# The squares of the expert rows move from GpSimd to ScalarE in a fused attention and mixture-of-experts kernel

## Chip, cores and metric

The kernel runs on one core of one Trainium2 chip. The metric is the device time of one execution in microseconds (us). Time before: 830.14 us, the median of 3 runs (828.5 to 830.5). Engines are named as in the profile: PE is TensorE (PEld its weight loads), DVE is VectorE, ACT is ScalarE, POOL is GpSimd, SP is SyncE.

## The reference, cut to what matters

The layer adds two branches to x of shape (1, 2048, 256), both computed from the layer norm xn of x. The attention branch holds a fast-weight memory that is updated after every 128 rows by five Newton-Schulz steps on three 64 x 64 matrices per head, and a sliding-window attention. The other branch is a routed mixture of 32 experts with a shared expert. The routed part is the one that the change touches:

```
def relu2(x):
    return jnp.square(jax.nn.relu(x))
...
x_lat = x @ fc1_w.T
h = relu2(jnp.einsum('tl,eil->eti', x_lat, w1))
h = h * cw.T[:, :, None]
y_lat = jnp.einsum('eti,eli->tl', h, w2)
routed = y_lat @ fc2_w.T
shared = relu2(x @ shared_up_w.T) @ shared_down_w.T
```

All data is float32.

## The kernel before

**Tiles.** The 2048 rows are worked in 16 tiles of 128 rows. The program of each engine is written out by hand, one block per engine, each with a function body(i, last) that is called for each tile i. Fifteen tiles have the full body, in which the projections and the routing of the next tile m = i + 1 are prepared beside the work of tile i; the last tile has a shorter one. Every engine works strictly through its own order, and waits on counting semaphores (wait_ge) stand in front of the instructions.

**The backbone of a tile** is the fast-weight update: k_side and grads give gradients, x_first scales them to X for two groups g of heads, and five Newton-Schulz iterations follow, each in four stages st. At stage 0 TensorE turns X (ns_turn, lines 699 and 700) and ScalarE copies the result to SBUF (xt, written XT<-CC); at stage 1 TensorE makes Gram products from XT (ns_gram, CC<-XT), which VectorE copies to Am; at stages 2 and 3 TensorE makes two more products (CC<-Am, CC<-X,Mp) and VectorE makes Mp and the next X, with GpSimd's aX = a * X as its addend. After the last iteration VectorE updates and renormalises the weights Wn (update, renorm), TensorE turns them (turn_w) and ScalarE copies them to WT (w_T). Everything else is hung between the stages by a table `fill` in each engine's body: `fill = {1: [...], 2: [...]}` names what is issued after stage 1, stage 2 and so on, 20 stages in all.

**The experts** go in eight steps u of four experts each. For each step:
- TensorE: h_up(i, u) writes 128 x 512 to the one PSUM bank HB; it waits for e_hr, the relu of the step before.
- ScalarE: h_relu(i, u) writes HB to the SBUF tile hr[u % 2] and counts e_hr.
- GpSimd: h_sq(i, u) squares it to hq[u % 2] and counts e_hq. It waits for e_hr, and for e_y of step u - 2, because y_down(i, u - 2) reads the buffer that it overwrites.
- TensorE: y_down(i, u) multiplies hq with the second expert weights into the one PSUM bank YB and counts e_y. It waits for e_hq and for e_acc of the step before.
- ScalarE (y_first, step 0) or VectorE (y_acc, line 1328) adds YB, times the routing weight, to acc and counts e_acc.

The steps are spread over the stages. Where they stand decides what waits for what, so here is the order in the full body. On TensorE:

```
h_up(i, 3)
fill = {2: [lambda: q_out(i), lambda: prep_turn(m)], 3: [lambda: y_down(i, 2)],
        4: [lambda: prep_qk(m)], 5: [lambda: prep_qk_more(m)], 6: [lambda: prep_v(m)],
        7: [lambda: h_up(i, 5)], 8: [lambda: y_down(i, 3), lambda: prep_mom(m)],
        9: [lambda: prep_turn_v(m), lambda: h_up(i, 6)], 10: [lambda: y_down(i, 4)],
```

with y_down(i, 1) right after the first ns_turn of group 0 and h_up(i, 4) right after the first ns_gram of group 0; y_down 5, 6 and 7 come after stages 13, 15 and 17. On ScalarE, before the stages: k_side, gate_sig, y_first(i), h_relu(i, 2), shared_relu(i), h_relu(i, 3); then

```
fill = {1: [lambda: h_relu(i, 4)], 2: [lambda: q_out(i), lambda: prep_xnT(m)],
        5: [lambda: prep_qk(m)], 6: [lambda: prep_v(m)], 7: [lambda: h_relu(i, 5), lambda: prep_small(m)],
        8: [lambda: prep_sq8(m)], 9: [lambda: prep_vT(m), lambda: h_relu(i, 6), to_exp],
```

where the xt copies of an iteration stand at its stage 0, that is before fill 0, 4, 8, 12 and 16; h_relu(i, 7) follows stage 14. After the stages come h_relu(m, 0), y_T(i), h_relu(m, 1) and w_T. to_exp and to_sigmoid (lines 567 and 570) load ScalarE's tables for exp and ln, and those for sigmoid.

Names in rows: to and tsq are q_out's copies (VectorE's q_ms, line 1199, reads tsq), xnT is prep_xnT's, M<-wall is the projection of the next tile (it reads xnT), sgs is prep_small's sigmoid (prep_mom on TensorE and the routing read it), sq<-sl is prep_sq8's square (VectorE's prep_ss8, line 1020, reads it), gs is a step of the routing (line 1272), dhb and dga are products of k_side on VectorE (lines 1094 and 1088) that the gradients read. Line 426 is ScalarE's helper a(), line 629 TensorE's helper mm(), line 285 GpSimd's power().

Of the kernel before, what the change touches and what calls it, by code (L numbers as in the profile page):

```python
# [27 lines left out]
ALU = mybir.AluOpType  # L28
ACT = mybir.ActivationFunctionType
# [17 lines left out]
NU = E // EU  # L47
# [26 lines left out]
def build(nc, x, wall_d, rows_d, wo, fast_d, affine_d, fc1T, fc2T, e1T, e2T, upT, downT, ident_d, fixed_d, out):  # L74
# [3 lines left out]
    with ExitStack() as ctx:  # L78
        def sb(name, shape):
            return ctx.enter_context(nc.sbuf_tensor(name, shape, F32))  # L80

        def bank(name):
            return ctx.enter_context(nc.psum_tensor(name, [P, 512], F32))

        def sem(name):
            return ctx.enter_context(nc.semaphore(name))
# [102 lines left out]
        hr = [sb(f"hr{b}", [P, EU, P]) for b in range(2)]  # L189
        hq = [sb(f"hq{b}", [P, EU, P]) for b in range(2)]  # L190
# [11 lines left out]
        HB = bank("HB")  # L202
# [30 lines left out]
        e_h, e_hr, e_hq, e_y, e_acc = (sem(n) for n in ("h", "h_relu", "h_sq", "y", "acc"))  # L233
# [41 lines left out]
        @block.gpsimd  # L275
        def _(pool):

            win_scores = Expect(pool, e_as, "win_scores", first=2)
            win_pv = Expect(pool, e_av, "win_pv", first=2)
            win_raw = Expect(pool, e_rawv, "win_raw", first=3)  # L280
            win_vw = Expect(pool, e_win, "win_vw", first=5, step=2)
            pool.wait_ge(e_init, 1)

            def power(dst, src, expo, n):
                return pool.tensor_tensor(dst, src, expo[:, 0:n], ALU.pow)  # L285

            def prep_rstd(m):
                pool.wait_ge(e_veps, m + 1)
                power(rstd[:, 0:1], rstd[:, 1:2], neghalf, 1).then_inc(e_rstd, 1)

            def prep_n8(m):
                pool.wait_ge(e_ss8, m + 1)
                power(r8[:, 1, :], r8[:, 0, :], half, 8).then_inc(e_n8, 1)

            def prep_kl(m):

                pool.wait_ge(e_lr, m + 1)
                for g in range(G):
                    pool.wait_ge(e_dw[g], m)
                kk = qkn[:, D:2 * D].rearrange("p (h c) -> p h c", c=HD)  # L300
                vv = sl[:, 2 * D:3 * D].rearrange("p (h c) -> p h c", c=HD)
                for dst, src, n in ((kl0, kk, 0), (kl2, kk, 2), (vl1, vv, 1)):
                    ins = pool.tensor_tensor(dst[:, :, :], src, lr[:, :, n:n + 1].to_broadcast([P, NH, HD]), ALU.mult)
                ins.then_inc(e_kl, 1)

            def window(m, known):

                if known:
                    pool.wait_ge(e_as, m)
                    pool.wait_ge(e_av, m)  # L310
                    pool.wait_ge(e_rawv, m + 1)
                else:
                    win_scores.wait()
                    win_pv.wait()
                    win_raw.wait()
                pool.tensor_copy(akT[:, :, 0, :], akT[:, :, 1, :])
                pool.tensor_copy(vw[:, 0, :], vw[:, 1, :]).then_inc(e_win, 1)

                if known:
                    pool.wait_ge(e_win, 2 * m + 1)  # L320
                else:
                    win_vw.wait()
                pool.tensor_copy(vw[:, 1, :], raw[:, 2 * D:3 * D]).then_inc(e_win, 1)

            def restore_mask():

                pool.wait_ge(e_sm, 1)
                pool.wait_ge(e_later, 16 * NLATER)
                pool.tensor_copy(mask[:, 0, :], mask_prev[:, :]).then_inc(e_mask, 1)

            def k_u(i, g):
                pool.wait_ge(e_kc[g], i + 1)
                pool.tensor_tensor(kt[g][:, 3, :], ks[g][:, 1, :], ks[g][:, 2, :], ALU.mult).then_inc(e_ku[g], 1)  # L333

            def ss_pow(i, g):
                pool.wait_ge(e_sst[g], 3 * i + 1)
                power(r3[g][:, 2, :], r3[g][:, 1, :], half, 3).then_inc(e_pw[g], 1)

            def ax(i, g, it):
                pool.wait_ge(e_x[g], (NI + 1) * i + it + 1)  # L340
                pool.tensor_tensor(aX[g][:, :, :].rearrange("p w c -> p (w c)"),  # L341
                                   X[g][:, :, :].rearrange("p w c -> p (w c)"), a_tile[:, it, :],
                                   ALU.mult).then_inc(e_ax[g], 1)

            def row_pow(m, g):

                pool.wait_ge(e_rn[g], m + 1)
                power(r3[g][:, 4, :], r3[g][:, 3, :], half, 3).then_inc(e_rp[g], 1)

            def rms_pow(i):  # L350
                pool.wait_ge(e_msq, 2 * i + 2)
                power(r4[:, 1, :], r4[:, 0, :], neghalf, 4).then_inc(e_rms, 1)

            def shared_sq(i):
                pool.wait_ge(e_ur, i + 1)
                pool.tensor_tensor(us[:, :, :], ur[:, :, :], ur[:, :, :], ALU.mult).then_inc(e_us, 1)

            def h_sq(i, u):
                pool.wait_ge(e_hr, NU * i + u + 1)
                if u > 1 or not (isinstance(i, int) and i == 0):  # L360
                    pool.wait_ge(e_y, NU * i + u - 1)
                b = u % 2
                pool.tensor_tensor(hq[b][:, :, :], hr[b][:, :, :], hr[b][:, :, :], ALU.mult).then_inc(e_hq, 1)  # L363

            def body(i, last):
                if last:
                    h_sq(i, 1)
                    h_sq(i, 2)
                    shared_sq(i)
                    h_sq(i, 3)  # L370
                    rms_pow(i)
                    for u in range(4, NU):
                        h_sq(i, u)
                    return
                m = i + 1
                first = i == 0
                k_u(i, 0)
                k_u(i, 1)
                h_sq(i, 1)
                for g in range(G):  # L380
                    ss_pow(i, g)
                prep_rstd(m)
                h_sq(i, 2)
                fill = {0: [lambda: shared_sq(i)], 1: [lambda: h_sq(i, 3)], 3: [lambda: rms_pow(i)],
                        4: [lambda: h_sq(i, 4)], 9: [lambda: prep_n8(m), lambda: h_sq(i, 5)],
                        12: [lambda: h_sq(i, 6)], 14: [lambda: h_sq(i, 7)], 16: [lambda: window(m, first)],
                        17: [lambda: prep_kl(m)]}
                if first:
                    fill[13] = [restore_mask]
                for st in range(4 * NI):  # L390
                    if st % 4 == 0:
                        for g in range(G):
                            ax(i, g, st // 4)
                    for f in fill.get(st, []):
                        f()
                for g in range(G):
                    row_pow(m, g)
                h_sq(m, 0)

            prep_rstd(0)  # L400
            for g in range(G):
                row_pow(0, g)
            prep_n8(0)
            window(0, True)
            prep_kl(0)
            h_sq(0, 0)

            body(0, False)
            for i in range(1, LAST):
                body(i, False)  # L410
            body(LAST, True)


        @block.scalar
        def _(act):
# [9 lines left out]
            def a(out_, in_, func, **kw):  # L425
                return nc.scalar.activation(out_, in_, func, **kw)  # L426
# [80 lines left out]
            def h_relu(i, u):  # L507
                act.wait_ge(e_h, NU * i + u + 1)
                if u > 1 or not (isinstance(i, int) and i == 0):
                    act.wait_ge(e_hq, NU * i + u - 1)  # L510
                a(hr[u % 2][:, :, :].rearrange("p s t -> p (s t)"), HB[:, :], ACT.Relu).then_inc(e_hr, 1)

            def y_first(i):

# [453 lines left out]
        def _(dve):  # L968
# [165 lines left out]
            def ns_m(i, g, it):  # L1134

                _, b, c = NS[it]
                dve.wait_ge(e_prod[g], 3 * NI * i + 3 * it + 2)
                nc.vector.scalar_tensor_tensor(Mp[g][:, :, :].rearrange("p w c -> p (w c)"),  # L1138
                                               Am[g][:, :, :].rearrange("p w c -> p (w c)"), b / c, CA[g][:, 0:3 * HD],
                                               ALU.mult, ALU.add).then_inc(e_mp[g], 1)  # L1140
# [313 lines left out]
```

## Time and profile before

| | before |
|---|---|
| median of 3 runs | 830.14 us |
| profiled execution, time | 830.14 us |
| its span | 828.1 us |
| PE busy | 780.7 us (94%) |
| DVE busy | 714.6 us (86%) |
| POOL busy | 406.8 us (49%) |
| ACT busy | 354.0 us (43%) |
| squares of expert rows on POOL | 128, 137.1 us |
| relus of expert rows on ACT | 128, 76.1 us |
| mean granted PE clock | 0.996 |

The span is the time from the first to the last instruction of the profiled execution; the time of the execution is 2.04 us longer. An engine's busy time says how much of the span it works, not whether the span would be shorter if it worked less: for that one needs the chain that ended last and the waits in the timeline of a single tile. A timeline row gives the start in us from the span's start, the duration in us, engine, line, operation, output<-inputs and count; brackets hold how long the engine was idle before it and whose result ended that. Consecutive like instructions are merged in one row.

### The profile page before, as it was taken

What the parts mean: (1) busy time and instruction counts of PE and PEld (TensorE: products, weight loads), DVE (VectorE), ACT (ScalarE), POOL (GpSimd) and SP (SyncE); (2) the same over time, 40 slices, a digit from 0 to 9 for tenths busy, and PEclk for the clock granted to TensorE, in tenths of its full rate; (3) what the DMA queues carried; (4) which work ended last, traced back from release to release, by engine and by line L of the source; (5) the groups of instructions that cost most, each with busy time, mean ns of one, the idle gap of its engine ahead of it and who ended that gap; (6) DMA issues with size and microseconds to landing.
All of it is one profiled execution on the core that took longest, in us unless ns stands there. A gap on an engine that the chain in (4) does not pass through costs nothing.

```text
span 828.1 us, 24889 instructions
## 1 busy us (share of the span) xinstructions
PE 780.7 (94%) x9776; PEld 668.5 (81%) x9776; DVE 714.6 (86%) x2592; ACT 354.0 (43%) x868; POOL 406.8 (49%) x535
## 2 busy tenths in 40 slices
PE   3899999999999999999999999999999999999997
PEld 1888888888888888878888788887888888888886
DVE  4789898898988979889798897988979889898876
ACT  2544344443444434444344444444444444434533
POOL 1654555445454454544555445544465444655442
PEclk9899999999999999999999999999999999999999
DMA  8100000000000000000000000000000000000000
GB/s 321 54 3 14 9 2 21 3 13 9 2 21 2 14 8 2 21 2 15 8 3 20 2 15 9 3 21 2 15 8 2 21 2 15 8 2 15 2 15 7
DMA packets 9811, 15.09 MB, mean 18 GB/s; under 512 B 1120, under 2 KB 8928, under 8 KB 9440
## 3 DMA queue, kind: packets, MB, share of 16 engines
q1 hardware_dynamic: 7904, 7.80, 3.2%
q10 hardware_dynamic: 1792, 5.70, 1.8%
q8 instruction: 78, 1.28, 0.6%
q14 instruction: 37, 0.30, 0.1%
HBM read 11.41 MB, written 2.10 MB: 16 GB/s over the span
## 4 chain that ended last, share of the span: by engine, by line
PE 53%; DVE 33%; issue 6%; ACT 5%; POOL 2%; DMA 1%; SPq 0%; DVEq 0%
PE CC L629 18%; PE M L629 13%; PE HB L629 8%; DVE acc L1328 8%; PE YB L629 8%; DVE Wn L1175 4%; DVE Mp L1138 2%; DVE dhb L1094 2%; DVE X L1146 2%; PE CC L699 2%; DVE Am L1131 2%; POOL r L285 2%; DVE sm L1233 1%; DMA rows<-in_rows 1%; PE CC L700 1%
## 5 line engine op out<-in xcount | busy, mean ns | idle before, releaser
L363 POOL TENSOR_TENSOR hq<-hr 128x512 f32<-128x512 f32 x128 | 137.1, 1071 | 71.9 <-ACT hr L426 71.9
L285 POOL TENSOR_TENSOR r<-r,half 128x3 f32<-128x3 f32 (+1 forms) x78 | 77.9, 1011 | 155.1 <-DVE r L1116 67.9
L629 PE MATMUL HB<-xlT,e_s 128*128 128x128 f32 x1024 | 143.0, 283 | 0.4 <-ACT xlT L426 0.4
L629 PE MATMUL YB<-e_s,hq 128*128 128x128 f32 x1024 | 141.3, 281 | 1.8 <-DVE acc L1328 0.8
L629 PEld LDWEIGHTS HB<-xlT,e_s 128*128 128x128 f32 x1024 | 126.7, 193 | 6.8 <-ACT xlT L426 0.7
L1328 DVE SCALAR_TENSOR_TENSOR acc<-YB,cw,acc 128x128 f32<-128x128 f32 x448 | 125.4, 342 | 7.9 <-PE YB L629 7.9
L341 POOL TENSOR_TENSOR aX<-X,a_tile 128x192 f32<-128x192 f32 x150 | 92.9, 640 | 79.9 <-DVE X L1146 79.9
L426 ACT ACTIVATE hr<-HB 128x512 f32<-128x512 f32 x128 | 76.1, 594 | 128.5 <-PE HB L629 128.5
L629 PEld LDWEIGHTS YB<-e_s,hq 128*128 128x128 f32 x1024 | 124.2, 191 | 7.4 <-issue 4.1
L629 PEld LDWEIGHTS CC<-X,Mp 64*64 64x64 f32 x1800 | 58.3, 135 | 23.6 <-issue 11.3
L629 PEld LDWEIGHTS CC<-Am 64*64 64x64 f32 x1800 | 59.5, 134 | 21.8 <-DVE Am L1131 18.2
L426 ACT ACTIVATE XT<-CC 128x256 f32<-128x256 f32 x150 | 50.8, 381 | 59.7 <-PE CC L700 59.5
L629 PE MATMUL CC<-X,Mp 64*64 64x64 f32 x1800 | 68.6, 222 | 7.6 <-DVE Mp L1138 7.6
L629 PE MATMUL CC<-Am 64*64 64x64 f32 x1800 | 69.8, 223 | 1.9
L1146 DVE SCALAR_TENSOR_TENSOR X<-CC,aX 128x192 f32<-128x192 f32 x150 | 51.3, 352 | 13.4 <-PE CC L629 13.3
L629 PE MATMUL M<-wall,xnT 128*128 128x512 f32 (+1 forms) x128 | 56.9, 551 | 3.6 <-DMA rows<-in_rows 3.6
L629 PEld LDWEIGHTS CC<-XT 64*64 64x64 f32 x1800 | 43.2, 133 | 20.7 <-ACT XT L426 14.7
L1131 DVE COPY Am<-CC 128x192 f32<-128x192 f32 x150 | 48.4, 347 | 9.3 <-PE CC L629 8.3
L1138 DVE SCALAR_TENSOR_TENSOR Mp<-Am,CC 128x192 f32<-128x192 f32 x150 | 49.8, 351 | 7.2 <-PE CC L629 3.6
L629 PE MATMUL CC<-XT 64*64 64x64 f32 x1800 | 55.6, 232 | 0.0
L699 PE MATMUL CC<-ident,X 128*64 128x128 f32 x150 | 39.7, 281 | 0.0
L333 POOL TENSOR_TENSOR kt<-ks 128x128 f32<-128x128 f32 x30 | 13.7, 459 | 51.0 <-ACT ks L426 51.0
(180 smaller groups left out, 1525.3 us busy)
## 6 DMA issues: line engine op xcount, KB each, us to landing
xa<-in_x SPq DMA_DIRECT2D x16, 128.0 KB, 2.1
e_s<-in_e1T ACTq DMA_DIRECT2D x1, 2048.0 KB, 12.7
e_s<-in_e2T ACTq DMA_DIRECT2D x1, 2048.0 KB, 19.3
xr<-in_x SPq DMA_DIRECT2D x16, 128.0 KB, 2.2
out<-ot SPq DMA_DIRECT2D x16, 128.0 KB, 1.7
wall<-in_wall SPq DMA_DIRECT2D x1, 820.0 KB, 7.1
up_s<-in_upT ACTq DMA_DIRECT2D x1, 512.0 KB, 15.9
down_s<-in_downT ACTq DMA_DIRECT2D x1, 512.0 KB, 20.0
```

Of the source, the lines that this page charges most:

```text
L285: return pool.tensor_tensor(dst, src, expo[:, 0:n], ALU.pow)
L341: pool.tensor_tensor(aX[g][:, :, :].rearrange("p w c -> p (w c)"), X[g][:, :, :].rearrange("p w c -> p (w c)"), a_tile[:, it, :], ALU.mult ...
L363: pool.tensor_tensor(hq[b][:, :, :], hr[b][:, :, :], hr[b][:, :, :], ALU.mult).then_inc(e_hq, 1)
L426: return nc.scalar.activation(out_, in_, func, **kw)
L629: return pe.matmul(out_, lhsT, rhs, start=start, stop=stop)
L699: pe.transpose(CA[g][0:HD, 0:P], X[g][:, 0, :], ident[:, :])
L1094: tt(dhb[g][:, :], kt[g][:, 0, :], dhi[g], ALU.mult)
L1131: nc.vector.tensor_copy(Am[g][:, :, :], CC[g][:, 0:6 * P].rearrange("p (w c) -> p w c", w=3)[:, :, 0:HD])\
L1138: nc.vector.scalar_tensor_tensor(Mp[g][:, :, :].rearrange("p w c -> p (w c)"), Am[g][:, :, :].rearrange("p w c -> p (w c)"), b / c, CA[g][ ...
L1146: nc.vector.scalar_tensor_tensor(X[g][:, :, :].rearrange("p w c -> p (w c)"), CB[g][:, 0:3 * HD], NS[it][2], aX[g][:, :, :].rearrange("p w ...
L1175: ins = nc.vector.tensor_scalar(Wn[g][:, w, :], Wn[g][:, w, :], r3[g][:, 5, w:w + 1], nrm[g][:, w:w + 1], ALU.mult, ALU.mult)
L1328: ins = nc.vector.scalar_tensor_tensor(acc[:, e, :], y, w, acc[:, e, :], ALU.mult, ALU.add)
```

## The change

ScalarE squares each expert step's rows right after its relu: hr stays the relu's output, hq the square's. GpSimd's h_sq is removed from its body, in all its places. h_relu's relu now waits on ScalarE for e_y of step u - 2 as well, the wait that stood before the square on GpSimd, and the square waits for ScalarE's own relu through e_hr. TensorE's, VectorE's and SyncE's programs stay as they are.

```
-            def h_sq(i, u):
-                pool.wait_ge(e_hr, NU * i + u + 1)
-                if u > 1 or not (isinstance(i, int) and i == 0):
-                    pool.wait_ge(e_y, NU * i + u - 1)
-                b = u % 2
-                pool.tensor_tensor(hq[b][:, :, :], hr[b][:, :, :], hr[b][:, :, :], ALU.mult).then_inc(e_hq, 1)
-
             def body(i, last):
                 if last:
-                    h_sq(i, 1)
-                    h_sq(i, 2)
                     shared_sq(i)
-                    h_sq(i, 3)
                     rms_pow(i)
-                    for u in range(4, NU):
-                        h_sq(i, u)
                     return
...
-                h_sq(i, 1)
                 for g in range(G):
                     ss_pow(i, g)
                 prep_rstd(m)
-                h_sq(i, 2)
-                fill = {0: [lambda: shared_sq(i)], 1: [lambda: h_sq(i, 3)], 3: [lambda: rms_pow(i)],
-                        4: [lambda: h_sq(i, 4)], 9: [lambda: prep_n8(m), lambda: h_sq(i, 5)],
-                        12: [lambda: h_sq(i, 6)], 14: [lambda: h_sq(i, 7)], 16: [lambda: window(m, first)],
+                fill = {0: [lambda: shared_sq(i)], 3: [lambda: rms_pow(i)],
+                        9: [lambda: prep_n8(m)], 16: [lambda: window(m, first)],
                         17: [lambda: prep_kl(m)]}
...
                 for g in range(G):
                     row_pow(m, g)
-                h_sq(m, 0)
...
             prep_kl(0)
-            h_sq(0, 0)
...
                 act.wait_ge(e_h, NU * i + u + 1)
                 if u > 1 or not (isinstance(i, int) and i == 0):
                     act.wait_ge(e_hq, NU * i + u - 1)
-                a(hr[u % 2][:, :, :].rearrange("p s t -> p (s t)"), HB[:, :], ACT.Relu).then_inc(e_hr, 1)
+                    act.wait_ge(e_y, NU * i + u - 1)
+                flat = "p s t -> p (s t)"
+                a(hr[u % 2][:, :, :].rearrange(flat), HB[:, :], ACT.Relu).then_inc(e_hr, 1)
+                act.wait_ge(e_hr, NU * i + u + 1)
+                a(hq[u % 2][:, :, :].rearrange(flat), hr[u % 2][:, :, :].rearrange(flat), ACT.Square).then_inc(e_hq, 1)
```

## Rows read from the trace of the kernel before

**Rows 1.** The profile page: busy time of the engines; the ending chain's shares by engine.
```profile
PE 780.7 (94%) x9776; PEld 668.5 (81%) x9776; DVE 714.6 (86%) x2592; ACT 354.0 (43%) x868; POOL 406.8 (49%) x535
...
PE 53%; DVE 33%; issue 6%; ACT 5%; POOL 2%; DMA 1%; SPq 0%; DVEq 0%
```

**Rows 2.** Timeline of one steady tile around u = 4: start us, duration us, engine, line, operation.
```profile
351.23 0.38 ACT L426 ACTIVATE to<-M 128x256 f32<-128x256 f32 x1 [1.45 <-PE M L629]
...
351.77 0.39 ACT L426 ACTIVATE xnT<-M 128x256 f32<-128x256 f32 x1
...
352.19 1.16 PE L629 MATMUL YB<-e_s,hq 128*128 128x128 f32 x8
...
353.62 1.02 PE L629 MATMUL M<-wall,xnT 128*128 128x512 f32 x2
```

**Rows 3.** Groups by line and form: count, busy us, mean ns, idle us before, releaser.
```profile
L363 POOL TENSOR_TENSOR hq<-hr 128x512 f32<-128x512 f32 x128 | 137.1, 1071 | 71.9 <-ACT hr L426 71.9
...
L426 ACT ACTIVATE hr<-HB 128x512 f32<-128x512 f32 x128 | 76.1, 594 | 128.5 <-PE HB L629 128.5
...
L567 ACT ACT_TABLE_LOAD x15 | 19.2, 1283 | 0.3
...
L426 ACT ACTIVATE sq<-sl 128x512 f32<-128x512 f32 x16 | 10.2, 639 | 0.4 <-DVE sl L1010 0.4
```

**Rows 4.** Timeline around the expert square of u = 1 on GpSimd.
```profile
338.83 1.09 POOL L363 TENSOR_TENSOR hq<-hr 128x512 f32<-128x512 f32 x1
338.92 1.06 PE L629 MATMUL YB<-e_s,hq 128*128 128x128 f32 x8
338.94 1.12 DVE L1094 TENSOR_TENSOR dhb<-kt,ks 128x128 f32<-128x128 f32 x1
...
340.62 0.30 PE L629 MATMUL CC<-kl,dga 128*64 128x64 f32 x2 [0.64 <-DVE dga L1088]
```

**Rows 5.** Instructions that touch dhb, then gs, on VectorE: ns min/median/max.
```profile
L1094 DVE TENSOR_TENSOR dhb<-kt,ks x30: 275/702/1124, 30.5 to 751.6; 128x128 f32<-128x128 f32 x30
...
L1272 DVE TENSOR_TENSOR gs<-g x16: 165/653/662, 20.5 to 779.3; 128x4 f32<-128x4 f32 x16
```

**Rows 6.** Timeline around u = 5 in the same tile.
```profile
360.37 0.60 ACT L426 ACTIVATE hr<-HB 128x512 f32<-128x512 f32 x1 [1.27 <-PE HB L629]
...
360.60 1.06 PE L629 MATMUL YB<-e_s,hq 128*128 128x128 f32 x8
360.86 0.23 ACT L426 ACTIVATE sgs<-z 128x40 f32<-128x40 f32 x1
...
362.19 0.69 DVE L1020 TENSOR_REDUCE r<-sq 128x8 f32<-128x512 f32 x1 [0.94 <-ACT sq L426]
```

**Rows 7.** Timeline around u = 3 in the same tile.
```profile
346.32 0.60 ACT L426 ACTIVATE hr<-HB 128x512 f32<-128x512 f32 x1 [0.30 <-PE HB L629]
...
346.40 1.06 PE L629 MATMUL YB<-e_s,hq 128*128 128x128 f32 x8
...
346.81 0.38 ACT L426 ACTIVATE XT<-CC 128x256 f32<-128x256 f32 x1
...
347.61 0.46 PE L629 MATMUL CC<-XT 64*64 64x64 f32 x12
```

**Rows 8.** Timeline around u = 6 in the same tile.
```profile
364.58 1.13 PE L629 MATMUL YB<-e_s,hq 128*128 128x128 f32 x8
...
367.87 0.66 ACT L426 ACTIVATE XT<-CC 128x256 f32<-128x256 f32 x2 [2.01 <-PE CC L700]
...
368.42 0.69 PE L629 MATMUL CC<-XT 64*64 64x64 f32 x24
...
369.89 0.63 DVE L1131 COPY Am<-CC 128x192 f32<-128x192 f32 x2
```

**Rows 9.** Timeline after u = 1 of the next tile, on ScalarE.
```profile
386.32 0.66 ACT L426 ACTIVATE WT<-CC 64x192 f32<-64x192 f32 x2
```

**Rows 10.** Windows of the last 8 us: engines busy us (instructions), TensorE's granted clock, DMA.
```profile
820.00:828.00 8.00, 4.41 (x22) 2.89 (x20) 3.09 (x11) 0.28 (x1) 0.00 (x0) 1.00 0.05 16
```

## The prediction

> **What bounds the kernel now.** I read the page's busy shares and its chain first. TensorE is busy for 94% of the span and the chain that ended last is 53% TensorE, 33% VectorE and only 5% ScalarE and 2% GpSimd [rows 1]. The reader should see that the engine that is relieved (GpSimd, 49% busy) and the engine that is loaded (ScalarE, 43%) are both far from full: the change will not be decided by their sums but by where TensorE or VectorE has to wait for them. So I next read the timeline of one steady tile. It repeats: the copy to<-M stands at 351.23 us [rows 2] and again at 402.57, so a tile takes 51.34 us, and there are 15 tiles with a full body and a shorter last one. The stretches from 346 to 360 us in this tile are TensorE back to back; from 361 to 373 us VectorE's queue sets the pace, with TensorE following.
>
> **What is removed.** 128 squares on GpSimd of 1.07 us each [rows 3], eight per tile. GpSimd is nearly off the chain, so its own time is worth nothing. What may be worth something is VectorE's. The product dhb takes 1.12 us at 338.94 while GpSimd squares from 338.83 to 339.92 [rows 4], and it ends just after it; over the run the same instruction takes 275 ns at the least and 702 at the median, since only the first of each pair meets a square [rows 5]. I read this as VectorE held back while GpSimd works. Two such places lie on the path of the end:
> - dhb: TensorE ends its product y_down(i,0) at 338.92 + 1.06 = 339.98, but starts the gradients only at 340.62, because VectorE is behind [rows 4]. With dhb at 0.28 us VectorE is 0.84 earlier, and TensorE can start at 339.98: **-0.64 us**, the whole gap. Bounds: 0 (if GpSimd is not the cause) and -0.64, since TensorE has no more to give there.
> - gs in the routing, within VectorE's own stretch: 653 ns at the median against 165 at the least [rows 5]: **-0.49 us**. Bounds 0 and -0.49, plus up to 1 us more per tile if other stretched instructions count too. I take none of those: where I found them, TensorE's queue was the later one.
>
> **What is added, by duration.** One Square per expert step, SBUF to SBUF, 128x512. The kernel has this form already (sq<-sl): 639 ns, against 594 for the relu [rows 3]. The square first waits for the relu to end. A following instruction of ScalarE starts about 0.11 us before the end of the one before it: the relu of 360.37 ends at 360.97, sgs starts at 360.86 [rows 6]. I allow 0.03 us for each hand-over. So relu and square together hold the queue for 0.60 + 0.03 + 0.53 = 1.16 us where the relu alone held it for 0.49: 0.67 more, 128 times, 86 us of ScalarE, which would then be about half busy. That alone is cheap; in most places ScalarE is waiting for TensorE anyway.
>
> **What is added, by waiting.** The relu of step u now also waits until y_down(u-2) has ended (e_y). Before, that wait stood in front of GpSimd's square, where nobody else queued. Now it stands in front of ScalarE's relu, and everything behind it on ScalarE waits as well. So I compared, for each u, where ScalarE reaches the relu and where TensorE reaches y_down(u-2). For u = 0, 1, 2 and 7 the product is long over. For u = 3, 4, 5 and 6 it lies later in TensorE's queue than the point where ScalarE now stands.
> - **u = 3.** y_down(i,1) comes after the first turn of X: 346.40 to 347.46. The relu ran at 346.32, before it, and XT, which the first Gram product needs, at 346.81 [rows 7]. Now: relu from 347.49, square from 348.12, XT from 348.65 to 349.03 (an XT takes 0.38), Gram product from 349.06 instead of 347.61: **+1.45 us**, with TensorE idle and the X iteration standing.
> - **u = 4.** y_down(i,2) ends at 352.19 + 1.16 = 353.35. Relu from 353.38, square from 354.01, to from 354.54; from to to xnT it is 0.54 us as now, so xnT runs from 355.08 to 355.47. The projection M<-wall needs xnT and stands ahead of the next Gram product on TensorE: 355.50 instead of 353.62 [rows 2]: **+1.88 us**. Next behind it, q_ms on VectorE gets tsq late, but ends before the delayed Gram product does.
> - **u = 5.** y_down(i,3) ends at 361.66. Relu from 361.69, square from 362.32, sgs from 362.85 instead of 360.86 [rows 6]: **+1.99 us**. Behind sgs stand the two XT and the square sq of the next tile, for which VectorE's reduction at 362.19 already waits today; TensorE's prep_mom waits for sgs too. So the delay goes into the stretch that VectorE sets, in full.
> - **u = 6.** y_down(i,4) ends at 365.71. Relu 365.74, square 366.37, the table load of 1.28 us [rows 3] from 367.02, lr_exp from 368.34, XT from 368.49 instead of 367.87; the Gram product starts at 368.90 instead of 368.42. VectorE takes the product up only at 369.89, when its other work is done [rows 8], so I count **+0.05 us**; if the cover were gone it would be 0.48.
> - **u = 1.** The square of step 1 now stands in front of the two WT copies, the first of which starts at 386.32, at once behind the relu [rows 9]. It costs the first copy 0.57 us; the second and TensorE's q_side come out about **+0.2 us** later, because they waited for a turn of Wn that VectorE now delivers a little earlier. Bounds 0 and 0.67.
>
> u = 0, 2 and 7 I cost at nothing: ScalarE waits for TensorE right behind them, and the wait covers 0.67 us.
>
> **The sum** per tile: 1.45 + 1.88 + 1.99 + 0.05 + 0.2 - 0.64 - 0.49 = +4.44 us; 15 tiles give +66.6. Start and last tile together: about -0.5, as stretched VectorE instructions there outweigh two squares on the path. The profiled execution has a span of 828.1 us and a time of 830.14, which is also the median of the three; so 828.1 + 66.6 - 0.5 + 2.04 = **896 us**, 7.9% slower.
>
> **The table sets.** There is one place where the existing rows cannot speak. Step 7 (and 4 to 7 of the last tile) squares while the tables for exp and ln are loaded; in the trace Square runs only under the sigmoid tables, while relu and copy run under both with no load ahead of them. The Trainium skill, page ScalarE: Activation LUTs, section on table sets, says that cheap functions appear in every set and names relu, copy, identity and abs, not square; by its rule a function outside the active set gets a load ahead of it. No row here shows which holds for Square.
>
> **The rivals.**
> 1. *The waits don't bite and the change is faster.* If the three relu steps found their y_down ended, only -0.64 - 0.49 + 0.2 = -0.93 us per tile would be left: 830 - 14 = 816 us. That needs ScalarE to be later than TensorE at u = 3, 4, 5; the rows show it earlier at u = 3 and u = 5 (relu at 346.32 and 360.37, y_down only ends at 347.46 and 361.66), and at u = 4 the relu stands ahead of to, which ran at 351.23, before y_down(i,2) began at 352.19. It decides once the stalls sum to under 0.93 us per tile. Chance 0.04.
> 2. *One stall is absorbed*, by slack that TensorE's full queue hides from me: 1.45 to 1.99 us less per tile, so 866 to 874 us. For it: VectorE gets through its queue while TensorE stands. Against: in-order queues wait for exactly these results. 0.08.
> 3. *GpSimd was not what stretched VectorE.* Then the two gains vanish: +1.13 us per tile, 17 more, 913 us. The coincidence of the ends speaks against it. 0.05.
> 4. *Square needs another table set.* Step 7 would pay two loads of 1.28 us, out and back, in front of lr_ln and prT, which TensorE waits for soon after: 2 to 2.56 us per tile, 30 to 38 more, 926 to 934 us. 0.03.
> 5. *TensorE's clock falls* in the new gaps. At the end of this run TensorE is busy for only 4.41 of 8 us, and the granted clock there is 1.00 [rows 10]; a tile of 55.8 us with the same work stays at about 87% busy. Should it fall, the time would be well over 913. 0.02.
>
> My own forecast has 0.78, with a range of its own of 884 to 908. With the parts of rivals 2 and 3 that lie nearest, the range is 878 to 912. About 0.3%, 2.5 us, is what can be told from no change: faster 0.04, the same 0.01, slower 0.95.
>
> **What would show it.** In the profile of the changed kernel: GpSimd down by about 137 us; ScalarE up by some 80; dhb at 0.28 us and gs at 0.17; the relu idle before it released by YB and not by HB in three places of every tile; TensorE idle before CC<-XT and before M<-wall, where it hardly waits now; VectorE idle before L1020 over 0.94 us; a tile of about 55.8 us; no more than the 34 table loads. I am wrong if XT follows its turn as closely as now, or if the idle time of TensorE grows by less than 3 us per tile.

## The result and the profile after

The changed kernel takes 927.76 us (median of 4 runs, 925.93 to 928.29) against 830.32 for the kernel before in the same comparison: ratio 1.117, 95% interval 1.115 to 1.119. It is 97 us slower, where 66 were forecast; the time lies outside the range of 878 to 912.

The page of the changed kernel: busy times, granted clock in 40 slices, chain, and the two expert operations on ScalarE.

```profile
PE 806.5 (87%) x9776; PEld 689.6 (75%) x9776; DVE 665.9 (72%) x2592; ACT 422.8 (46%) x996; POOL 276.2 (30%) x407
...
PEclk9999999999999999989999999999999989999999
...
PE 72%; ACT 20%; issue 4%; DVE 3%; DMA 1%; ACTq 0%; SPq 0%; DVEq 0%
...
L409 ACT ACTIVATE hr<-HB 128x512 f32<-128x512 f32 x128 | 76.4, 597 | 274.2 <-PE YB L616 200.1
...
L409 ACT ACTIVATE hq<-hr 128x512 f32<-128x512 f32 x128 | 80.6, 630 | 4.0
```

Three things answer to [rows 1] and [rows 3]. ScalarE's share of the chain goes from 5% to 20% though it is busy only 69 us more. Its 128 relus wait 200.1 us for YB, which they never waited for before. And TensorE is busy 26 us more with the same 9776 instructions, so some of them ran slower. GpSimd loses 131 us, and VectorE is busy 49 us less with the same 2592 instructions.

Now one steady tile, first on ScalarE around u = 3 and u = 5, then the same tile on TensorE.

```profile
326.89 0.60 ACT L409 ACTIVATE hr<-HB 128x512 f32<-128x512 f32 x1 [1.56 <-PE YB L616]
327.51 0.63 ACT L409 ACTIVATE hq<-hr 128x512 f32<-128x512 f32 x1
328.05 0.64 ACT L409 ACTIVATE XT<-CC 128x256 f32<-128x256 f32 x2
...
346.27 0.60 ACT L409 ACTIVATE hr<-HB 128x512 f32<-128x512 f32 x1 [2.69 <-PE YB L616]
346.90 0.63 ACT L409 ACTIVATE hq<-hr 128x512 f32<-128x512 f32 x1
347.43 0.22 ACT L409 ACTIVATE sgs<-z 128x40 f32<-128x40 f32 x1
```

```profile
325.71 1.06 PE L616 MATMUL YB<-e_s,hq 128*128 128x128 f32 x8
328.47 0.46 PE L616 MATMUL CC<-XT 64*64 64x64 f32 x12 [1.48 <-ACT XT L409]
...
333.05 1.16 PE L616 MATMUL YB<-e_s,hq 128*128 128x128 f32 x8
336.46 1.12 PE L616 MATMUL M<-wall,xnT 128*128 128x512 f32 x2 [1.81 <-ACT xnT L409]
...
345.09 1.06 PE L616 MATMUL YB<-e_s,hq 128*128 128x128 f32 x8
```

The order product, relu, square, XT or sgs, next product is the one of the forecast. From the end of y_down(i,1) at 326.77 to the relu it is 0.12 us, where the forecast allowed 0.03; the Gram product starts at 328.47, 1.70 us after y_down(i,1) ends; before it was 0.15 [rows 7]. And then the part that the forecast gave 0.02: the windows of this tile, and of the next one around u = 5. Columns are the stretch, its length, busy us and instructions of PE, PEld, DVE, ACT, POOL, then TensorE's granted clock, the DMA share and GB/s.

```profile
334.00:336.00 2.00, 0.65 (x6) 0.41 (x5) 0.00 (x0) 1.64 (x4) 0.00 (x0) 1.00 0.00 0
336.00:338.00 2.00, 1.54 (x24) 0.79 (x26) 1.64 (x6) 0.95 (x4) 1.14 (x2) 0.97 0.02 4
338.00:340.00 2.00, 2.00 (x12) 0.68 (x6) 1.84 (x6) 0.00 (x0) 0.98 (x2) 0.50 0.00 0
340.00:342.00 2.00, 2.00 (x27) 1.56 (x27) 0.76 (x3) 1.09 (x2) 0.00 (x0) 0.68 0.03 8
342.00:344.00 2.00, 2.00 (x31) 1.45 (x30) 0.63 (x3) 0.66 (x2) 0.14 (x1) 1.00 0.00 0
```

```profile
404.00:406.00 2.00, 0.49 (x12) 0.48 (x13) 0.00 (x0) 1.90 (x6) 0.00 (x0) 1.00 0.00 0
406.00:408.00 2.00, 2.00 (x31) 1.88 (x28) 1.46 (x5) 0.90 (x2) 0.69 (x1) 0.53 0.00 0
408.00:410.00 2.00, 2.00 (x29) 1.77 (x28) 1.18 (x7) 0.00 (x0) 0.94 (x1) 0.61 0.01 4
```

TensorE is busy for 0.65 of 2 us in the gap of u = 4, and soon after runs for over 3 us at half the clock (1.2 instead of 2.4 GHz); in the next tile the same follows the gap of u = 5. The mean clock of the run is 0.963, of the kernel before 0.996. The difference, 0.963 over 925.5 us against 0.996 over 828.1, is some 62 us more at the lower level.

Not every gap is followed by a fall. The next windows are four tiles of this kernel, each from one start of M<-wall behind the gap of u = 4 to the next; the work in them is the same.

```profile
48.70:104.93 56.23, 49.44 (x637) 42.68 (x637) 42.29 (x166) 26.52 (x64) 18.05 (x27) 1.00 0.03 9
104.93:162.32 57.39, 51.11 (x637) 43.95 (x638) 42.48 (x166) 26.54 (x64) 17.78 (x26) 0.97 0.03 9
162.32:220.11 57.79, 50.99 (x638) 43.43 (x638) 42.52 (x166) 26.53 (x64) 17.76 (x26) 0.97 0.03 9
220.11:279.07 58.96, 52.50 (x637) 44.82 (x637) 42.66 (x166) 26.52 (x64) 17.77 (x26) 0.94 0.03 8
```

The first has no fall (clock 1.00) and takes 56.23 us. The second has one behind the gap of u = 5 (at 116 us), the third one behind the gap of u = 4 (at 164 us), the fourth both (at 222 and 232 us): 1.16, 1.56 and 2.73 us more. Over the 15 full tiles each of the two gaps is followed by a fall 9 times, though it has the same length in every tile (1.81 and 1.55 us). What decides which 9 is not shown.

### The profile page after: what moved, and what is told of

The parts are those of the page before. It is cut to its first block, busy times and chain, and to the rows that moved or that the text cites. A ratio compares the mean times of both kernels' runs of the same rounds, so it can differ in the third digit from the quotient of the medians.

```text
span 925.5 us, 24763 instructions
## 1 busy us (share of the span) xinstructions
PE 806.5 (87%) x9776; PEld 689.6 (75%) x9776; DVE 665.9 (72%) x2592; ACT 422.8 (46%) x996; POOL 276.2 (30%) x407
## 4 chain that ended last, share of the span: by engine, by line
PE 72%; ACT 20%; issue 4%; DVE 3%; DMA 1%; ACTq 0%; SPq 0%; DVEq 0%
PE CC L616 23%; PE M L616 19%; PE HB L616 14%; PE YB L616 12%; ACT hr L409 5%; ACT hq L409 3%; ACT L557 2%; ACT L554 2%; ACT XT L409 2%; DVE acc L1315 1%; DMA rows<-in_rows 1%; PE M L774 1%; DVE Am L1118 1%; ACT prT L409 1%; ACT WT L409 1%
## 5 line engine op out<-in xcount | busy, mean ns | idle before, releaser
L409 ACT ACTIVATE hr<-HB 128x512 f32<-128x512 f32 x128 | 76.4, 597 | 274.2 <-PE YB L616 200.1
L341 POOL TENSOR_TENSOR aX<-X,a_tile 128x192 f32<-128x192 f32 x150 | 95.5, 657 | 195.5 <-DVE X L1133 195.5
L616 PE MATMUL HB<-xlT,e_s 128*128 128x128 f32 x1024 | 150.5, 293 | 0.4 <-ACT xlT L409 0.4
L616 PEld LDWEIGHTS HB<-xlT,e_s 128*128 128x128 f32 x1024 | 133.7, 202 | 6.9 <-ACT xlT L409 0.7
L616 PE MATMUL M<-wall,xnT 128*128 128x512 f32 (+1 forms) x128 | 67.4, 636 | 30.7 <-ACT xnT L409 27.2
L616 PEld LDWEIGHTS CC<-Am 64*64 64x64 f32 x1800 | 68.6, 151 | 28.3 <-issue 15.6
L616 PE MATMUL CC<-XT 64*64 64x64 f32 x1800 | 57.9, 236 | 31.3 <-ACT XT L409 31.3
L616 PE MATMUL CC<-Am 64*64 64x64 f32 x1800 | 81.4, 240 | 1.8
L409 ACT ACTIVATE hq<-hr 128x512 f32<-128x512 f32 x128 | 80.6, 630 | 4.0
L285 POOL TENSOR_TENSOR r<-r,neghalf 128x4 f32<-128x4 f32 x16 | 16.2, 1014 | 131.5 <-DVE r L1188 131.5
L616 PEld LDWEIGHTS M<-wall,xnT 128*128 128x128 f32 x128 | 23.4, 214 | 41.6 <-ACT xnT L409 30.7
```

Of the source, the lines that this page charges most:

```text
L616: return pe.matmul(out_, lhsT, rhs, start=start, stop=stop)
```

## The experiments

**1. Products that nobody reads, in TensorE's gaps.** This keeps every wait and takes only the idleness away. The products go to columns of a bank that nothing else uses.

```
+            def keep_busy(n):
+                for _ in range(n):
+                    mm(CB[0][:, 3 * P:4 * P], ident[:, :], fc1_s[:, 0, :])
...
+                            if st == 1 and g == 0:
+                                keep_busy(4)
                             ns_gram(g)
...
+    4: [lambda: keep_busy(6), lambda: prep_qk(m)], 5: [lambda: prep_qk_more(m)]
+    8: [lambda: y_down(i, 3), lambda: keep_busy(5), lambda: prep_mom(m)]
```

> The changed kernel, and TensorE gets matrix products whose result nobody reads in the three places where it now stands: 4 ahead of the first Gram product of group 0, 6 ahead of the projection M<-wall, 5 ahead of prep_mom (0.27 us each by the rows of YB, 1.06 us for four, so 1.1, 1.6 and 1.3 us of idle gaps of 1.5, 1.8 and 1.6 us). Every wait stays. Theory A (the waits cost what the forecast said, 4.4 us per tile, and the rest of the loss is TensorE's clock, which falls to 0.50 after the gaps): granted clock 0.99, time 892 to 902 us, a tile of 55.8 us. Theory B (the clock costs nothing because other engines set the pace where it is low; the stalls or squares themselves are dearer): clock up or not, the time stays at 925 or more.

Measured: 903.07 us, ratio 1.087 (1.085 to 1.089), clock 0.996. Adding 225 products, which are 450 matmul instructions in the trace (10226 against 9776), made the kernel 24.7 us faster than the changed one. Theory B falls. The time is 1 us above theory A's bracket, so the waits are a little dearer than forecast; a tile shows where. TensorE, and VectorE's reduction, of one tile of this kernel:

```profile
375.12 1.06 PE L616 MATMUL YB<-e_s,hq 128*128 128x128 f32 x8
377.88 0.46 PE L616 MATMUL CC<-XT 64*64 64x64 f32 x12 [0.59 <-ACT XT L409]
...
382.46 1.16 PE L616 MATMUL YB<-e_s,hq 128*128 128x128 f32 x8
385.86 1.12 PE L616 MATMUL M<-wall,xnT 128*128 128x512 f32 x2 [0.47 <-ACT xnT L409]
392.95 1.06 PE L616 MATMUL YB<-e_s,hq 128*128 128x128 f32 x8
...
431.36 1.06 PE L616 MATMUL YB<-e_s,hq 128*128 128x128 f32 x8
```

```profile
396.60 0.69 DVE L1013 TENSOR_REDUCE r<-sq 128x8 f32<-128x512 f32 x1 [3.01 <-ACT sq L409]
```

A tile is 431.36 - 375.12 = 56.24 us, as long as the changed kernel's own tile without a fall (56.23): so the products took away the falls and changed nothing else of its length. From start to start, in us:

| stretch | before | fillers | difference | forecast |
|---|---|---|---|---|
| y_down(i,1) to first Gram product | 1.21 | 2.76 | +1.55 | +1.45 |
| Gram product to y_down(i,2) | 4.58 | 4.58 | 0 | 0 |
| y_down(i,2) to M<-wall | 1.43 | 3.40 | +1.97 | +1.88 |
| M<-wall to y_down(i,3) | 6.98 | 7.09 | +0.11 | 0 |
| y_down(i,3) to the reduction | 1.59 | 3.65 | +2.06 | +1.99 |
| reduction to the next y_down(i,1) | 35.55 | 34.76 | -0.79 | -0.88 |
| tile | 51.34 | 56.24 | +4.90 | +4.44 |

The column before is from [rows 7], [rows 2] and [rows 6]. In the changed kernel itself the fourth stretch is 345.09 - 336.46 = 8.63 us: the stretch at half clock costs 1.54 us there. Nine such stretches and nine of 1.16 us behind the gap of u = 5 make 24.4 us, against the 24.7 given back.

**2. One gap filled at a time**, the 6 products of u = 4 alone and the 5 of u = 5 alone.

> The changed kernel with products that nobody reads in only one of its three gaps: 6 of them ahead of the projection M<-wall (behind the delayed copy of u = 4). The falls of the clock in the changed kernel come in pairs of places, some 2 us after this gap and about as long after the gap of u = 5. Theory A: the falls after this gap vanish, those near u = 5 stay; mean clock between 0.97 and 0.99, 908 to 918 us. Rival (any one gap less is enough, or the falls move to the other gap): 903 or 927 us.

> The changed kernel with 5 such products in the gap of u = 5 alone, ahead of prep_mom. Theory A: only the falls near u = 5 vanish, 908 to 920 us, clock 0.97 to 0.99. Rival as for the gap of u = 4: 903 or 927 us.

Measured: 913.53 us (1.100, 1.099 to 1.102), clock 0.981, and 916.30 us (1.103, 1.101 to 1.105), clock 0.979. They give back 14.2 and 11.5 us, together 25.7, against 24.7 with all gaps filled: the two gaps act nearly apart, and both bring the clock down. In these two kernels the gap of u = 3 (1.48 us) does so too, more rarely: the first has 7 falls behind the gap of u = 5 and one behind that of u = 3 (at 554 us), the second 7 behind the gap of u = 4 and two behind that of u = 3 (at 211 and 556 us).

**3. The wait alone.** The kernel before, with one line more.

```
                     act.wait_ge(e_hq, NU * i + u - 1)
+                    act.wait_ge(e_y, NU * i + u - 1)
```

> The kernel before with one line: the relu on ScalarE also waits for e_y of step u - 2. Squares stay on GpSimd. Theory A (the place of the wait is the loss): XT, to/xnT and sgs come 0.78, 1.21 and 1.32 us late per tile (the forecast's terms less 0.67 for the square), 3.3 us per tile, nothing of VectorE's gains: 875 to 885 us, plus up to 25 us if the clock falls too. Theory C (ScalarE's squares are the loss, the wait is cheap): 830 to 840 us.

Measured: 888.55 us, ratio 1.069 (1.068 to 1.071), clock 0.994. Without one square moved, the wait costs 58 us. Theory C falls. It is 3.6 us above the bracket without a fall of the clock. TensorE's three gaps in this kernel (us in total, times, longest):

```profile
PE M L630 <- ACT xnT L426: 17.4, 15, 1.2
PE M L630 <- ACT sgs L426: 14.7, 16, 1.3
PE CC L630 <- ACT XT L426: 12.4, 15, 0.8
```

In a full tile that is 1.16, 0.89 and 0.82 us, against 1.81, 1.55 and 1.48 in the changed kernel: shorter by about the square's 0.67 us. The granted clock from 30 to 850 us is 1.00, so no full tile has a fall; the 0.002 in the mean is one fall in the last tile. Gaps of this length did not bring the clock down.

**4. The squares alone.** Four hq buffers, so that e_y of step u - 4 does, and the relu waits for no e_y; all else as changed.

```
-        hq = [sb(f"hq{b}", [P, EU, P]) for b in range(2)]
+        hq = [sb(f"hq{b}", [P, EU, P]) for b in range(4)]
...
-                    act.wait_ge(e_y, NU * i + u - 1)
...
+                if u > 3 or not (isinstance(i, int) and i == 0):
+                    act.wait_ge(e_y, NU * i + u - 3)
```

> The changed kernel with four hq buffers instead of two; the relu no longer waits for e_y, the square waits for y_down of step u - 4, which is long over. All squares stay on ScalarE right behind their relus. Theory A: +0.28 us at XT behind u = 3, +0.67 at sgs behind u = 5, +0.2 at WT, -0.64 for dhb and -0.49 for gs: about 0 per tile, 822 to 838 us, clock 0.99. Theory C (ScalarE's squares are the loss): 900 us or more.

Measured: 823.81 us, ratio 0.992 (0.990 to 0.993), clock 0.996. From 928 to 824 us by two more buffers: the wait is the whole loss against the kernel before. The squares are not free where they stand, though: the kernel without any, in experiment 6, takes 799.17 us, 24.6 less. Part of that is TensorE waiting for ScalarE's copies (us in total, times, longest):

```profile
PE CC L617 <- ACT WT L409: 12.4, 14, 0.9
```

**5. One square out of the way.** The same with the square of u = 1 moved behind gate_sig.

> The kernel with four hq buffers, and the square of u = 1 alone moved from in front of the WT copies to behind gate_sig. Theory A: the copies start 0.5 to 0.6 us earlier and TensorE's idle time before CC<-WT (0.9 us per tile with four buffers) nearly goes: 811 to 816 us, from 823.8. Rival (that stretch is set by VectorE's Wn): 821 to 824 us.

Measured: 813.60 us, ratio 0.980 (0.978 to 0.981), and the wait is down:

```profile
PE CC L624 <- ACT WT L409: 3.0, 13, 0.2
```

Its place in front of the WT copies cost 10.2 us, 0.68 per tile, where I had charged 0.2.

**6. No squares at all**, y_down reads the relu's rows from four buffers, so the output lacks the square in the routed experts: the ceiling of what GpSimd's squares can cost.

> No squares at all: y_down reads the relu's rows from four hr buffers, so the output lacks the square in the routed experts. GpSimd does as little as in the changed kernel and ScalarE no more than before. It shows what GpSimd's squares cost the kernel before. Theory A: -0.64 us (dhb) and -0.49 us (gs) per tile and some 0.2 us for WT: 810 to 816 us. Rival (GpSimd was not what stretched VectorE): 828 to 832 us, dhb still at 1.1 us.

Measured: 799.17 us, ratio 0.962 (0.960 to 0.963). GpSimd's squares cost the kernel before 31.7 us, 2.1 per tile, and not the 1.13 that I had counted. That they, and not something else, hold VectorE back is tried next.

**7. Relu and square apart**, two hq buffers as changed. The relus stay and wait for no e_y; the squares, with the wait, stand where ScalarE is idle:

```
                 if u > 1 or not (isinstance(i, int) and i == 0):
                     act.wait_ge(e_hq, NU * i + u - 1)
+                a(hr[u % 2][:, :, :].rearrange("p s t -> p (s t)"), HB[:, :], ACT.Relu).then_inc(e_hr, 1)
+
+            def h_sq(i, u):
+                flat = "p s t -> p (s t)"
+                act.wait_ge(e_hr, NU * i + u + 1)
+                if u > 1 or not (isinstance(i, int) and i == 0):
                     act.wait_ge(e_y, NU * i + u - 1)
-                flat = "p s t -> p (s t)"
-                a(hr[u % 2][:, :, :].rearrange(flat), HB[:, :], ACT.Relu).then_inc(e_hr, 1)
-                act.wait_ge(e_hr, NU * i + u + 1)
                 a(hq[u % 2][:, :, :].rearrange(flat), hr[u % 2][:, :, :].rearrange(flat), ACT.Square).then_inc(e_hq, 1)
...
                 gate_sig(i)
+                h_sq(i, 1)
                 y_first(i)
                 h_relu(i, 2)
+                h_sq(i, 2)
...
+                fill = {0: [lambda: h_sq(i, 3)], 1: [lambda: h_relu(i, 4)], 4: [lambda: h_sq(i, 4)], 2: [lambda: q_out(i), lambda: prep_xnT(m)],
...
+                        8: [lambda: prep_sq8(m), lambda: h_sq(i, 5)], 9: [lambda: prep_vT(m), lambda: h_relu(i, 6), to_exp],
+                        11: [lambda: lr_exp(m), lambda: h_sq(i, 6)], 12: [lambda: prep_qkT(m)],
+                        13: [lambda: probs(i)], 14: [lambda: h_relu(i, 7), lambda: h_sq(i, 7), lambda: lr_ln(m)], 15: [lambda: probs_T(i), to_sigmoid],
...
                 y_T(i)
+                h_sq(m, 0)
```

> The changed kernel with two hq buffers as it is, but with relu and square apart: the relus stand where they are and wait for no e_y; the wait goes with the square, and the squares stand where ScalarE is idle and y_down of u - 2 is over: u = 0 behind y_T, 1 behind gate_sig, 3 after the XT copies of stage 0, 4 after those of stage 4, 5 behind prep_sq8, 6 behind lr_exp, 2 and 7 behind their relus. Theory A (only the place of the wait and of three squares costs; ScalarE has the room): close to the kernel without squares at 799.2 us, so 799 to 806 us, clock 0.99. Rival (128 more instructions on ScalarE cost in themselves): 815 us or more.

Measured: 799.38 us, ratio 0.962 (0.961 to 0.964): 3.8% faster than the kernel before, 128 us faster than the changed one, and level with the kernel that does no squares. ScalarE around u = 3:

```profile
334.06 0.60 ACT L409 ACTIVATE hr<-HB 128x512 f32<-128x512 f32 x1 [0.30 <-PE HB L630]
334.56 0.38 ACT L409 ACTIVATE XT<-CC 128x256 f32<-128x256 f32 x1
335.46 0.38 ACT L409 ACTIVATE XT<-CC 128x256 f32<-128x256 f32 x1 [0.52 <-PE CC L701]
335.74 0.62 ACT L409 ACTIVATE hq<-hr 128x512 f32<-128x512 f32 x1
```

The relu waits for its product HB again, XT is next in the queue, and the square comes when nobody waits for ScalarE.

**8. One product back on GpSimd.** The kernel of 799.4 us, and once per tile GpSimd makes a 128x512 product of constant tiles in the place, and behind the waits, of one of its old squares.

```
+            def spare_sq(i, u):
+                pool.wait_ge(e_hr, NU * i + u + 1)
+                if u > 1 or not (isinstance(i, int) and i == 0):
+                    pool.wait_ge(e_y, NU * i + u - 1)
+                pool.tensor_tensor(spare[:, :, :], e1_s[:, 0:EU, :], e1_s[:, 0:EU, :], ALU.mult)
```

> The kernel with relu and square apart (799.4 us), and GpSimd again has one product of 128x512 per tile, from constant tiles into a spare one that nobody reads, in the place and behind the waits of its old square of u = 1. Theory A (such a product holds VectorE back, and costs what lies on the path of the end): dhb at 1.1 us again in group 0, 0.64 us per tile, 809 us (807 to 811). Rival: GpSimd's work is free, 799 to 800 us.

> The same, with the spare product in the place of the old square of u = 0, behind row_pow, where VectorE scales Wn. The forecast took this place as free, since TensorE's h_up(m, 1) ended no earlier than the scaled Wn. If that holds: 799 to 801 us. Now rather expected, since all squares on GpSimd cost 2.0 us per tile and not the 1.1 of the forecast: 0.4 to 0.7 us per tile, 805 to 810 us.

> The same, with the spare product in the place of the old square of u = 6, where VectorE makes gs. Forecast's term: 0.49 us per tile, 807 us (805 to 808), gs at 0.65 us again. Rival: it is free, 799 to 800 us.

Measured: 811.63 us for the place of u = 1, 807.01 for that of u = 0, 805.96 for that of u = 6. Against 799.38 that is 12.2, 7.6 and 6.6 us, 0.82, 0.51 and 0.44 per tile, and added up 26.5 of the 31.7 us. Of VectorE's groups only the one beside the product grows by more than 1 us over the run (dhb by 11.8, Wn by 10.9, gs by 7.4 us); the three rows are from the three kernels, ns min/median/max.

```profile
L1103 DVE TENSOR_TENSOR dhb<-kt,ks x30: 277/281/1124, 30.9 to 734.8; 128x128 f32<-128x128 f32 x30
```

```profile
L1184 DVE TENSOR_SCALAR Wn<-Wn,r,nrm x90: 306/312/1039, 74.8 to 775.5; 128x64 f32<-128x64 f32 x90
```

```profile
L1280 DVE TENSOR_TENSOR gs<-g x16: 167/650/653, 20.4 to 756.7; 128x4 f32<-128x4 f32 x16
```

The product shares no data with these instructions, so what they wait for is GpSimd's work itself. The rival that GpSimd is free falls in all three places.

## Why the prediction was wrong, step by step

**The direction and the mechanism were right.** The relu's wait for e_y holds up ScalarE's queue at u = 3, 4 and 5, and TensorE behind it. Experiments 3 and 4 show it from both sides: the wait without the squares costs 58 us, and with the squares but without the wait the kernel is 7 us faster than before.

**The three stalls** were sized +1.45, +1.88 and +1.99 us; with the clock held up they are +1.55, +1.97 and +2.06. The tenth that each lacks is the hand-over from y_down to the relu, for which I had allowed 0.03 us: the relu starts 0.12 us after the product's end at u = 3 and at u = 5 of the tile shown (326.77 to 326.89, 346.15 to 346.27).

**The step that failed is rival 5**, "TensorE's clock falls in the new gaps", chance 0.02. I read from the window of the last 8 us, 4.41 of them busy at a clock of 1.00 [rows 10], that such gaps are harmless, and the sum had no term for them. But that window ends with the run: it says nothing of what the clock would have done had there been work after it. The start of the same trace would have spoken against it. TensorE is busy for 1.94 of the first 10 us and 5.91 of the next, and then, busy again, it has a clock of 0.67 over 10 us, so some 6.6 us at the lower level:

```profile
10.00:20.00 10.00, 5.91 (x12) 2.76 (x12) 1.77 (x5) 3.15 (x8) 0.00 (x0) 0.98 1.01 409
20.00:30.00 10.00, 8.60 (x48) 7.90 (x48) 7.25 (x38) 7.25 (x16) 6.43 (x10) 0.67 0.36 128
```

The changed kernel shows gaps of 1.8 us followed by a stretch at 0.50, 1.54 us dearer where it could be read. Filling the gaps gives back 24.7 us, that is 1.6 per tile, and accounts for 24.7 of the 31.8 us between forecast and measurement. It was also priced without a number ("well over 913"), where the rows could have given one: the projection and Gram products behind the gap, at twice their time. The Trainium skill, page TensorE: Matmul & The Clock Gate, Part 1, says that an idle TensorE is granted 1.2 GHz and a busy one 2.4; the trace agrees on the two levels (0.50 and 1.00).

**The rest, 7 us, is mis-sized terms**, +4.90 per tile instead of +4.44. The three stalls make 0.26 of the difference and the stretch from M<-wall to y_down(i,3) 0.11. From the reduction to the next y_down(i,1) it is only 0.09, but there larger errors cancel, and that is luck:
- *gs, -0.49, and u = 6, +0.05.* gs takes 0.15 instead of 0.65 us in the filler kernel, but with VectorE early the cover behind u = 6 is gone, the case for which the sum named 0.48. TensorE and then VectorE stand there:

```profile
403.36 0.73 PE L616 MATMUL CC<-XT 64*64 64x64 f32 x24 [0.45 <-ACT XT L409]
403.85 0.64 DVE L1124 COPY Am<-CC 128x192 f32<-128x192 f32 x2 [0.17 <-PE CC L616]
```

Counted from the reduction, this Gram product comes at 6.76 us where it was 6.23 ([rows 6] and [rows 8]), and the product CC<-X,Mp after it at 10.44 instead of 10.62. So the two terms together gave 0.18, where the sum had 0.44.
- *u = 1, +0.2.* Measured 0.68 (experiment 5, with four hq buffers; TensorE's wait for WT, 12.4 us, is the same in the changed kernel). I had the WT copies wait for a turn of Wn and so hide most of the square; but with VectorE freed, Wn is early and the copies themselves are what TensorE waits for.
- *Wn, taken at nothing.* The spare product in that place costs 0.51 us per tile (experiment 8). I looked only at group 0, where TensorE's h_up(m, 1) ends as late; group 1's scaling stands behind it in VectorE's queue, and TensorE waits for that one. This gain and the losses above partly cancel: from the reduction to the next y_down(i,0) it is 28.11 us in the filler kernel and was 28.07, so +0.04, where the sum had -0.24.
- *dhb, -0.64.* 0.82 by the spare product, and 0.83 in the filler kernel: from y_down(i,0) to y_down(i,1) it is 6.65 us (368.47 to 375.12) instead of 7.48 ([rows 4] and [rows 7]). The bound "TensorE has no more to give" went by the gradients of group 0 alone; those of group 1 come 0.80 us earlier in the filler kernel, counted from the reduction, while y_down(i,0) comes 0.04 later.

**Rival 3** (GpSimd didn't stretch VectorE) falls: dhb takes 275 to 280 ns in the changed kernel, with a median of 278 where it was 702 [rows 5], and the spare products bring each stretch back. **Rivals 1 and 2** fall: no stall was absorbed. **Rival 4**, the tables: the changed kernel has the same table loads as before, 34 in all, these two kinds among them.

```profile
L554 ACT ACT_TABLE_LOAD x15 | 19.2, 1283 | 0.3
L557 ACT ACT_TABLE_LOAD x15 | 19.2, 1283 | 0.3
```

So Square runs under the tables for exp and ln too; the rule on table sets of the Trainium skill's page ScalarE: Activation LUTs, whose list of functions in every set does not name square, holds for it as for relu and copy.

## What to carry to other kernels

When work moves between engines, move its waits to the instruction that needs them and no earlier: a wait that stood in front of nobody on GpSimd stood in front of the whole backbone on ScalarE. Compare, step by step, where the new engine reaches the wait with where the other engine releases it; either reorder (799 us) or add buffers (824 us) until the wait is met on arrival. And when a change opens gaps on a TensorE that was busy throughout, price the clock as a term of its own: here it was a quarter of the loss.

## What the hardware showed that I had not expected

- TensorE that stood idle for 1.5 to 1.8 us three times per tile, and was busy for most of the rest, was granted half the clock for over 3 us afterwards, once or twice in 14 of the 15 full tiles; 225 products whose result nobody reads made the kernel 24.7 us faster.
- In the kernel with the wait alone the gaps are shorter by about 0.67 us (1.16 us at most in a full tile), and no full tile has a fall. So a small cut of a gap can save more than its own length; the two kernels differ in the place of the squares too, and no run changed the length of a gap alone.
- A GpSimd product of 1.1 us stretches single VectorE instructions beside it from 0.28 to 1.12 us (128x128), from 0.31 to 1.04 (128x64) and from 0.17 to 0.65 (128x4), though they touch other data; eight such per tile cost 2.1 us of a tile's 51.3.
